# Attention and gated low-rank layer on Trainium2: two PSUM banks each for attention values and filler matmuls, and the gate weights on another engine

## What is computed

```python
q = LN(x) @ Wq + bq                       # 16 heads of 64
k = (LN(x) @ Wk + bk) @ Wl + bl
v = (LN(x) @ Wv + bv) @ Wl + bl
z = softmax(q k^T / 8) v @ Wo + bo
x2 = x + LN(z)
x3 = LN(x2)
gate = softmax(x3 @ router_W^T + router_b)   # 6 experts, the two largest kept
w = top2(gate) / (sum(top2(gate)) + 1e-6)
y = x3 @ base_W^T + base_b + shared rank-16 path
y += sum over experts e of w[e] * (x3 @ A_e^T) @ B_e^T      # rank 16
out = x2 + LN(y)
```

## Time and profile before

| | us |
|---|---|
| three runs, median (lowest to highest) | 1542.91 (1541.95 to 1544.85) |
| profiled execution | 1545.22 |
| span of its slowest core (core 1) | 1543.7 |
| spans of the eight cores | 1526.3 to 1543.7 |

### The profile page before, as it was taken

One profiled execution on the slowest core, in us unless ns is written; L12 is line 12 of the kernel. 1 busy time (PEld: TensorE's weight loads), 2 busy tenths in 40 slices (PEclk: granted clock), 3 DMA queues, 4 the chain that ended last, 5 costly groups with the idle time before them and its releaser, 6 DMA issues.

```text
span 1543.7 us, 43311 instructions; the slowest of 8 cores (1526.3 to 1543.7 us)
## 1 busy us (share of the span) xinstructions
PE 1352.1 (88%) x17136; PEld 829.8 (54%) x17136; DVE 663.4 (43%) x1603; ACT 1053.8 (68%) x1197; POOL 417.1 (27%) x573
## 2 busy tenths in 40 slices
PE   2699995999999999999968989998898798888873
PEld 1347563566656665655535555555555455555431
DVE  3422233333232323232225556555565455554555
ACT  2426773777777777777746778777787587688631
POOL 4200002101010101010014555555555444552521
PEclk9899997999999999999979999999999899999986
DMA  9910003202020211024622222212212211211110
GB/s 197 212 29 6 9 8 99 69 16 67 17 63 16 60 26 50 22 73 88 106 80 65 70 83 70 83 64 84 70 60 87 70 63 56 84 50 59 40 69 28
DMA packets 68422, 99.06 MB, mean 64 GB/s; under 512 B 29584, under 2 KB 47120, under 8 KB 67712
## 3 DMA queue, kind: packets, MB, share of 16 engines
q1 hardware_dynamic: 56224, 82.18, 16.8%
q0 software_dynamic: 11712, 13.06, 6.0%
q10 hardware_dynamic: 288, 1.05, 0.2%
HBM read 76.40 MB, written 32.93 MB: 71 GB/s over the span
## 4 chain that ended last, share of the span: by engine, by line
PE 73%; DVE 9%; issue 5%; DMA 5%; ACT 4%; POOL 3%; DVEq 0%; SPq 0%; POOLq 0%; ACTq 0%
PE fb L363 34%; PE sc L991 16%; PE av L1021 14%; PE fb L415 4%; ACT p_sb L1008 3%; DMA xst<-x 3%; DMA urow<-u_scr 2%; PE fb L709 1%; PE sc L363 1%; DVE y_sb L869 1%; DVE sta L246 1%; DVE sty L246 1%; DVE x L743 1%; PE fb L787 1%; PE av L363 1%
## 5 line engine op out<-in xcount | busy, mean ns | idle before, releaser
L1008 ACT ACTIVATE p_sb<-sc 128x1024 bf16<-128x1024 f32 x1024 | 991.8, 1025 | 361.6 <-PE sc L993 355.6
L1021 PEld LDWEIGHTS av<-v_sb,p_sb 128*128 128x128 bf16 x8192 | 324.2, 98 | 128.8 <-issue 41.1
L1021 PE MATMUL av<-v_sb,p_sb 128*128 128x65 bf16 x8192 | 345.4, 195 | 19.9 <-DVE u_sb L1049 18.7
L991 PE MATMUL sc<-q_sb,k_sb 64*128 64x256 bf16 x2048 | 334.5, 275 | 16.4 <-ACT p_sb L1008 14.2
L993 PE MATMUL sc<-q_sb,k_sb 64*128 64x256 bf16 x2048 | 336.7, 276 | 0.0
L991 PEld LDWEIGHTS sc<-q_sb,k_sb 64*128 64x128 bf16 x2048 | 145.2, 95 | 86.2 <-issue 47.4
L993 PEld LDWEIGHTS sc<-q_sb,k_sb 64*128 64x128 bf16 x2048 | 141.5, 95 | 0.0
L363 PE MATMUL fb<-bw_sb,x3fm 128*128 128x512 bf16 x496 | 139.6, 398 | 0.1
L254 POOL TENSOR_SCALAR rsa<-sta 128x1 f32<-128x1 f32 x32 | 7.2, 226 | 482.1 <-DVE sta L250 387.6
L363 PE MATMUL fb<-wo_sb,ut 128*128 128x512 bf16 x496 | 134.5, 389 | 2.7 <-DVE ut L240 2.7
L363 PE MATMUL fb<-xfm,wq_sb 128*128 128x512 bf16 x496 | 126.9, 385 | 0.9 <-DVE xfm L240 0.9
(11 more groups left out here) (175 smaller groups left out, 1439.0 us busy)
## 6 DMA issues: line engine op xcount, KB each, us to landing
xst<-x SPq DMA_DIRECT2D x64, 512.0 KB, 5.1
out<-y_sb SPq DMA_DIRECT2D x32, 512.0 KB, 3.0
urow<-u_scr SPq DMA_DIRECT2D x30, 256.0 KB, 3.8
u_scr<-u SPq DMA_DIRECT2D x64, 64.0 KB, 1.9
q_scr<-kq SPq DMA_DIRECT2D x32, 128.0 KB, 2.3
q_sb<-q_scr SPq DMA_DIRECT2D x4, 1024.0 KB, 7.2
u_scr<-u_sb SPq DMA_DIRECT2D x8, 512.0 KB, 3.5
wl_sb<-wl POOLq DMA_DIRECT2D x2, 1024.0 KB, 43.7
```

The source lines that it names most:

```text
L991: t.matmul(sc[slot][:, ci * 256:(ci + 1) * 256], k_sb[0:64, j, c * 128:(c + 1) * 128], qa[0:64], start=True, stop=True, tile_position=(0, 0))
L1008: exp_tok[g] = P.op("S", lambda a: a.activation(ps[:], sc[slot][:], AF.Exp, bias=-SHIFT, scale=1.0), tok, av_tok.get(g - 4))
L1021: r = t.matmul(av[:, o:o + 65], ps[:, h * 512 + ci * 256 + qh * 128:h * 512 + ci * 256 + (qh + 1) * 128], v_sb[:, j, c * 130 + h * 65:c * ...
```

## The change

- PSUM: `av` becomes two banks (4 and 5), used by units in turn; the filler ring in the steps shrinks from three banks to two (6 and 7).
- The order of one tile's part of the list becomes: load_u(n+1); z(n) first half 8; gate_mul(n-2); tr3(n-1) 2; z(n) second half 8; tr_h(n-2) 0.25; y(n-2) first half 9; tr_u(n+1) 2; five quanta of y(n-2) second half; ln3(n); its other four; h(n-1) 1.84. A blank quantum of cost 8 in tile 0 is gone.
- Gate: one exponential of six logits; DVE takes the two largest of the exponentials; six small operations that were DVE's are made by POOL.
- `ln_rstd` leaves out its third POOL operation where POOL applies the norm, which then subtracts the mean and multiplies.
- `in1_ln` of sequence 1's tiles 0 and 1 stand within the fold of Wv, its x loads at the head of the list, and its first four `tr_in` at the head of each slice of head pair 2; 6 units of blank cost (4 x 1.0 of norms, 2.0) are gone.

```diff
-        fb = [... "fb%d" ... for i in range(3)]
+        av = [... "av%d" ... for i in range(2)]
+        fb = [... "fb%d" ... for i in range(2)]
...
         def ln_rstd(kind, slot, tok, nmr=False):
...
+            if not nmr:
+                return [tok, b]
...
+        def ln_apply(e, kind, slot, out, src, *toks):
+            s_, r_ = st[kind][slot], rs[kind][slot]
+            if e == "S":
+                return P.op("S", lambda a: a.activation(out, src, AF.Identity, bias=r_[:, 2:3], scale=r_[:, 1:2]),
+                            *toks)
+            return P.op("G", lambda g: g.tensor_scalar(out, src, s_[:, 12:13], r_[:, 1:2],
+                                                       ALU.subtract, ALU.mult), *toks)
...
         def head_pair(j):
             out = []
             for sl in range(4):
+                if j == 2:
+                    out += first[sl]
+                    if sl < 2:
+                        out.append((0.0, lambda sl=sl: in1_ln(sl + 2), None))
...
-        for tt in range(4):
-            ones.append([(1.0, lambda tt=tt: in1_ln(tt), None)])
-            if tt:
-                ones.append([(2.0, lambda tt=tt: tr_in(ln_of[1, tt - 1], 4, tt - 1), None)])
-        ones.append([(2.0, lambda: None, None)])
-        ones.append([(2.0, lambda: tr_in(ln_of[1, 3], 4, 3), None)])
+        first = [[(2.0, lambda tt=tt: tr_in(ln_of[1, tt], 4, tt), None)] for tt in range(4)]
...
+        for t in range(3):
+            add(lambda t=t: pre_x(1, t))
...
+                if n == "v" and i in (2, 5):
+                    add(lambda i=i: in1_ln(i // 3))
...
         def gate_mul(n):
...
+            m = P.op("V", lambda v: v.max(g_[:, 24:32], g_[:, 16:24]), hm_tok[n], w_tok["lgpad"])
+            a = P.op("V", lambda v: v.tensor_tensor(g_[:, 12:13], g_[:, 24:25], g_[:, 25:26], ALU.add), m)
+            P.op("V", lambda v: v.max_index(i_[:], g_[:, 24:32], g_[:, 16:24]))
+            b = P.op("V", lambda v: v.scalar_tensor_tensor(...), a)
+            P.op("V", lambda v: v.reciprocal(g_[:, 46:47], g_[:, 13:14]), b)
+            c = P.op("V", lambda v: v.tensor_copy(g_[:, 14:16], i_[:, 0:2]))
+            P.op("G", lambda v: v.tensor_scalar(g_[:, 32:38], iota, ...), c)
+            d = P.op("G", lambda v: v.tensor_scalar(g_[:, 40:46], iota, ...))
+            e = P.op("G", lambda v: v.tensor_tensor(g_[:, 32:38], g_[:, 32:38], g_[:, 40:46], ALU.add), d)
+            w = P.op("G", lambda v: v.tensor_scalar(g_[:, 32:38], g_[:, 32:38], g_[:, 46:47], None, ALU.mult), e)
+            P.op("G", lambda v: v.tensor_copy(hm[s][:, 0:16], hs[s][:, 0:16]), hT_free[s])
+            hm_done[n] = P.op("G", lambda v: v.tensor_tensor(hm[s][:, 16:112]..., w)
...
         def pv(g):
...
-                            r = t.matmul(av[:, o:o + 65],
+                            r = t.matmul(av[u % 2][:, o:o + 65],
...
-            av_tok[g] = P.op("T", mm, exp_tok[g], vw, mul_tok.get(u - 1) if s == 0 else None,
-                             bfree[4] if g == 0 else None)
+            av_tok[g] = P.op("T", mm, exp_tok[g], vw, mul_tok.get(u - 2) if s == 0 else None,
+                             bfree[4 + u] if u < 2 and s == 0 else None)
...
-        ring["list"], ring["n"] = [5, 6, 7], 0
+        ring["list"], ring["n"] = [6, 7], 0
```

More of the change, by code:

```diff
@@ L250, in ln_aggr, with ln_rstd @@
             return P.op("V", lambda v: v.bn_aggr(o, i), *toks)
-        def ln_rstd(kind, slot, tok):
+        def ln_rstd(kind, slot, tok, nmr=False):
             s_, r_ = st[kind][slot], rs[kind][slot]
@@ L585, in build_nc @@
         ones = []
-        for t in range(3):
-            ones.append([(0.0, lambda t=t: pre_x(1, t), None)])
-        for tt in range(4):
-            ones.append([(1.0, lambda tt=tt: in1_ln(tt), None)])
-            if tt:
-                ones.append([(2.0, lambda tt=tt: tr_in(ln_of[1, tt - 1], 4, tt - 1), None)])
-        ones.append([(2.0, lambda: None, None)])
-        ones.append([(2.0, lambda: tr_in(ln_of[1, 3], 4, 3), None)])
+        first = [[(2.0, lambda tt=tt: tr_in(ln_of[1, tt], 4, tt), None)] for tt in range(4)]
         for sl in range(4):
@@ L717, in build_nc, with norm_add @@
         adds = []
-        def norm_add(n, out, y, r_, x, rt, done, *toks):
+        def norm_add(n, kind, out, x, ag, done, *toks):
+            rt = ln_rstd(kind, n % 4, ag, state["tail"])
             if state["tail"]:
-                yt = P.op("S", lambda a: a.activation(out[:], y[:], AF.Identity, bias=r_[:, 2:3],
-                                                      scale=r_[:, 1:2]), rt)
+                yt = ln_apply("S", kind, n % 4, out[:], out[:], rt)
                 def add_x():
@@ L731, in norm_add @@
             else:
-                yt = P.op("G", lambda g: g.tensor_scalar(out[:], y[:], r_[:, 1:2], r_[:, 2:3], ALU.mult, ALU.add), rt)
+                yt = ln_apply("G", kind, n % 4, out[:], out[:], rt)
                 done(P.op("G", lambda g: g.tensor_tensor(out[:], out[:], x[:], ALU.add), yt, *toks))
@@ L793, in tr3 @@
             bfree[b] = x3_tok[n]
-        hm_tok = {}
+        hm_tok, hm_done = {}, {}
         def h_group(n):
@@ L892, in gated @@
             add(lambda: gate_mul(n), 0.0, lambda: n in hm_tok)
-        for n in range(NT - 2):
+        for n in range(NT):
+            cur = n < NT - 2
             if n + 1 < NT - 2:
                 add(lambda n=n: load_u(n + 1), 0.0, lambda n=n: u_ready(n + 1))
-            filler += z_group(n, 0)
-            if n > 0:
+            if cur:
+                filler += z_group(n, 0)
+            if n > 1:
+                gated(n - 2)
+            if 0 < n < NT - 1:
                 add(lambda n=n: tr3(n - 1), 2.0)
-            filler += z_group(n, 1)
+            if cur:
+                filler += z_group(n, 1)
             if n > 1:
                 add(lambda n=n: tr_h(n - 2), 0.25)
-            if n > 0:
-                filler += h_group(n - 1)
+                filler += y_group(n - 2, 0)
             if n + 1 < NT - 2:
                 add(lambda n=n: tr_u(n + 1), 2.0)
-            if n > 1:
-                filler += y_group(n - 2, 0)
-            if n == 0:
-                add(lambda: None, 8.0)
-            add(lambda n=n: ln3(n))
-            if n > 1:
-                filler += y_group(n - 2, 1)
-            if n > 0:
-                gated(n - 1)
-        e, f = NT - 4, NT - 3
-        add(lambda: tr_h(e), 0.25)
-        filler += y_group(e, 0)
-        add(lambda: tr3(f), 2.0)
-        filler += y_group(e, 1)
-        filler += h_group(f)
-        gated(f)
-        add(lambda: tr_h(f), 0.25)
-        filler += y_group(f, 0) + y_group(f, 1)
+            y1 = y_group(n - 2, 1) if n > 1 else []
+            filler += y1[:5]
+            if cur:
+                add(lambda n=n: ln3(n))
+            filler += y1[5:]
+            if 0 < n < NT - 1:
+                filler += h_group(n - 1)
         c, d = NT - 2, NT - 1
```

81 lines of the change are left out of this document (29 added, 52 removed).

## The result

The changed kernel takes 1645.8 to 1648.6 us, 1.068 times the kernel before (95% interval 1.066 to 1.070): 104 us slower, where 30 us faster was forecast, and 100 us above the top of the range.

What follows compares the result with a forecast made beforehand. TensorE was taken as the bound all along, with its stalls and the lower clock after them to win. Terms -22 -41 +50 +5 -21 -8 +0 +6.5 = -30.5 us took 1542.9 to 1512 us, range 1491 to 1547.

Steps and rivals of the forecast that it cites:

- The start of the tiles: At the first two tr3: 1.8 us more without the blank, 0.9 less without the third ln_rstd operation; sized 0.
- four places: Tiles 28 and 29 and twice in the tail, where nothing hides the longer gate chain before tr_h.
- The late-transfer rival: At tr_u: POOL's longer chain or the SP queue keeps urow late, half of 41 us stays; 1532 us, chance 0.14.
- The slower one: Rival at DVE's z and y evictions: filler-bank handovers cost more than the stalls they replace; 1563 at 0.9 us each, chance 0.15.
- values' second bank and two filler banks: At PSUM: stalls before the value matmuls go, -22 us; filler handovers cost +50, and +5 in sequence 0.
- tile order, with the blank: At tr_u, moved behind y's first half: nine more filler units cover the late transfer; -41 us.
- sequence 1's norms in the folds: Near 250 us: 15.1 us of stalls go, -15, and the lower clock after them, -6.
- gate on POOL: Between gate_mul and tr_h: chain 2.0 us longer, hidden in the steps, paid at tiles 28, 29 and the tail; +6.5.
- one rstd operation fewer ahead of the norm: In POOL's norm chain: 0.9 us shorter at the first tr3, elsewhere covered by POOL's idle half; 0.
- The handovers: Behind 880 us: big groups wait for evictions of their one filler bank; +43, and +7 for a busy DVE.
- the clock behind 880 us: TensorE's clock of 0.98 costs 12 us there; it partly recovers as longer stalls go, -8 us.
- the stall at 250 us: TensorE's wait for sequence 1's first norms, 15.1 us, forecast to go.

Runs made afterwards that it cites:

- e1: The changed kernel with POOL's norms back in the old form (multiply, add), all else kept: 1517.8 us, ratio 0.983.
- e2: The kernel before with nothing but POOL's norms changed to (subtract, multiply): 1715.2 us, ratio 1.111.
- e11: e1 with y's norm alone in the slow form (subtract, multiply): ratio 1.029.
- e6: e1 with the banks of before, one for the values and three for the filler: 1505.5 us, ratio 0.974.
- e7: e1 with the tile order of before, its blank of 8 units and its gate place included: ratio 0.991.
- e8: e1 with sequence 1's first norms and loads in one piece again at the head of their list: ratio 0.994.
- e5: e1 with the six gate operations on DVE instead of POOL: ratio 0.986.
- e14: The changed kernel with only its norm mended, as add (minus the mean), multiply: 1511.6 and 1513.5 us in two executions.
- e10: e6 with the norm as add, multiply, the mean negated on POOL ahead of the power: ratio 0.966.
- e4: e1 with POOL's four norms in four forms: (multiply, subtract), (add, multiply), subtract and multiply as two instructions, (multiply, add): 1638.1 us.
- e12: e1 with norms as (multiply, multiply), (add, add), multiply and add as two instructions, y's (multiply, add), for durations only: 1648.5 us.

## Why the prediction was wrong

**The step that failed** is the one on the norm, under "The start of the tiles". It costed the third `ln_rstd` operation that goes ("0.26 us, with its gap 0.44") and said "Elsewhere this operation is covered by POOL's idle half". What takes its place, 105 norms as (subtract, multiply) instead of (multiply, add), has no term in the sum. It was silently given the price of the old form. The trace of before has no `tensor_scalar` of this pair on POOL at 1024 columns, so it had to be bounded: from below by 1.19 us, from above by the nearest POOL row of that size, the additions of 2.35 us. Even the upper bound would have been too low, but it would have put 1.1 us into y's chain per tile and pointed at the gate behind it. The measured price is 3.80 us, and e1 and e2 show what it costs: 130 us in the changed kernel, 170 in the kernel before.

By the Trainium skill (GPSIMD Engine Reference, When to use GPSIMD) elementwise operations with one input run on GpSimd roughly at line rate, and two-input ones at about half of VectorE's speed; the first would have made the norm cheap in either form. The rows here differ, and the measurement decides: with one input and 1024 columns POOL takes 1.19, 2.87 or 3.80 us, according to the operations named. The prediction's estimate of 2.7 us for the gate's six operations, from twice their durations on DVE, was too high as well: they took 2.1. (Its 0.4 us more at four places would also be 1.6 us, not 1.)

**The cover that was gone.** "In the steps 10 units, 2.1 steps or 5 us, lie between `gate_mul` and `tr_h`, which hides it." The chain itself was sized well: POOL's part is 2.1 us in the timeline above (forecast 2.3). What was left out is what stands ahead of it in POOL's queue. The late-transfer rival says that the gate's work "stands behind y's norm in program order", and takes it as good for the store; it was not asked what y's norm, rstd and addition do to the gate. In e1, with fast norms, `tr_h` still waits 26.9 us instead of 12.5, and with y's norm alone slowed (e11) 78.4. DVE's half of the gate adds to it: in e1 it is often held up to the end of POOL's addition (last section), and POOL then waits for the rest of it, 0.79 us in the tile at 918 us. No rival named this place. The slower one put the loss at the filler banks; their waits stay at 17 us in the changed kernel.

**The terms that the runs sized:**

| part | forecast, us | measured, us | by |
|---|---|---|---|
| norm's form | no term | +130 | changed kernel, e1 |
| values' second bank and two filler banks | -22 +50 +5 = +33 | +14 | e6, e1 |
| tile order, with the blank | -41 | -11 | e7, e1 |
| sequence 1's norms in the folds | -21 | -16 | e8, e1 |
| gate on POOL | +6.5 | -4.6 | e5, e1 |
| one rstd operation fewer ahead of the norm | 0 | -5 (two executions); -12 with one values bank | e14, e1; e10, e6 |

The handovers were over-priced. The eviction waits are 25.9 us in 43 pieces in e1; with 0.16 each for the modelled ends 33 us, against 50. Their form was as forecast, pieces of at most 0.9 us, more than half of them `x`'s. The values' stalls were priced right: 19.9 us before, none after, 20.5 in e6. The order's stalls went as forecast too (2.3 us left), but they were partly another part's gain, and the new order pays 14 us of them back in handovers (e7). The prediction counted those under the banks; in the table they lower both rows, so the rows of the banks and of the order are not independent. The row on the rstd shows a second slip of the same step: shortening POOL's chain is worth much more than "0", since what TensorE waits for at `tr_h` is queued behind that chain. Without the form's price the measured rows add up to -23 us, and e14 stands some 30 below before; how the rest divides between the handovers that count twice, the clock behind 880 us (-8 in the forecast) and other effects of the parts on each other, the runs don't tell. That the forecast's 1512 and e14 agree comes of errors that cancel: forecast less measured, +19 on the banks, -30 on the order, +11 on the gate, -5 on the norms of sequence 1 and +5 on the rstd, none in all. So that agreement is luck.

**What held:** TensorE's stalls as the thing to read, the stall at 250 us and the low clock behind it gone, no idle time before the values, `tr_u` at 2.3 us, and the stalls of 5.8 and 6.1 us near the end before `tr_h` (e1).

## What to carry to other kernels

An edit that drops an instruction often rewrites its neighbour: every instruction whose operations change is a new one, and gets a price of its own or bounds from both sides, however alike its shape. On an engine that is half idle, ask what stands ahead of a short operation in its queue before you move one there that the bound engine waits for: here 75 us of longer norms ahead of the gate (e11) brought 51.5 us of idle time and 71 us in all. And when a profile names a releaser whose output the waiting instruction does not read, look at the instruction just before it on that engine.

## What the runs showed of the hardware

- POOL's `tensor_scalar` on 128x1024 has three prices by its pair of operations: 1.19 us, 2.86 to 2.88 and 3.79 to 3.80 (e4, e12). Two operations in one instruction can take less than half the time of one alone.
- Small operations cost about 0.1 us more on POOL than on DVE: a (compare, multiply) of 6 columns took 0.42 us there and 0.29 on DVE, the product of 96 columns 0.35 and 0.26.
- Small DVE operations can be held up by what runs on POOL. By the Trainium skill (SBUF — State Buffer, Who interferes with whom) the port that GpSimd shares with VectorE is locked for a whole instruction. The kernel before agrees: 21 of the gate's operations on L808, L825, L828 and L833 began while POOL ran a norm or an addition, 18 of them took over 0.12 us more than the shortest of their line, and all 18 ended within 0.05 us of POOL's instruction. The 2.1 us of the earlier trace rows are one of these, ending at 1479.79 where POOL's addition ends at 1479.77:

```profile
1477.43 2.34 POOL L733 TENSOR_TENSOR y_sb<-y_sb,x 128x1024 f32<-128x1024 f32 x1
1477.66 2.13 DVE L828 TENSOR_SCALAR gt<-gt 128x2 f32<-128x2 f32 x1
```

- The slow form holds DVE up less than the fast one. In e1 24 of 28 of the gate's sums (L821) that began within a norm or an addition of POOL were lengthened to its end. In the changed kernel 78 operations of the lines L805, L823 and L828 began within a norm of 3.80 us, and only 10 were lengthened, 4 of them to the norm's end and none past 0.85 us. Why, no run shows. None of DVE's 62 evictions of `x` took over 0.69 us in either kernel.
- With stalls of 3.5 us on average in 23 tiles (changed kernel, longest 6.0) or 5.5 us in 26 (e2, longest 7.0) the granted clock behind 880 us was 0.90 and 0.87, where it is 0.98 with a quarter of the changed kernel's idle time before `tr_h` (e1). TensorE's busy time, for the same 17136 matmuls, is 52 us longer in the changed kernel than in e1.
